# A fused decoder layer on one Trainium2 core: a prologue in halves, 26 weight pieces on GpSimd, and two steps of the end moved

## What is computed

```
x = layernorm(x + attn(x))        # causal, 32 heads of 16, with biases
x = layernorm(x + xattn(x, ctx))  # 32 query heads, 8 key/value heads of 128, rope, mask
x = layernorm(x + ffn(x))         # 4-bit weights, out = (silu(x Wg) * (x Wu)) Wd
```

## Time and profile before

| what | us |
|---|---|
| median of 3 runs | 992.58 (988.86 to 994.84) |
| the profiled execution: time / span | 994.55 / 992.7 |
| first matmul / first scores | 14.96 / 32.66 |
| self-attention, scores of step 0 to scores of step 56 | 154.0 |
| steps 56 to 71 | 73.0 |
| cross-attention and feed-forward, from 259.64 to the end | 733.1 |
| TensorE / VectorE / ScalarE / GpSimd busy in the span | 912.0 / 729.7 / 463.7 / 365.3 |

### The profile page before, as it was taken

One profiled execution on the slowest core, in us unless ns is written; L12 is line 12 of the kernel. 1 busy time (PEld: TensorE's weight loads), 2 busy tenths in 40 slices (PEclk: granted clock), 3 DMA queues, 4 the chain that ended last, 5 costly groups with the idle time before them and its releaser, 6 DMA issues.

```text
span 992.7 us, 17835 instructions
## 1 busy us (share of the span) xinstructions
PE 912.0 (92%) x6552; PEld 520.5 (52%) x6552; DVE 729.7 (74%) x1190; ACT 463.7 (47%) x1335; POOL 365.3 (37%) x330
## 2 busy tenths in 40 slices
PE   3876899888789999999999999999998989999997
PEld 2555677544345555545555555555554544444443
DVE  5685989877577877859787687787788655898343
ACT  3665788641145545535554454554545533333100
POOL 2152122103345444534554455446556230231011
PEclk9997999889999999999999999999999999999999
DMA  6634442210001101012002003004111010220001
GB/s 198 222 133 145 154 119 65 84 67 1 1 1 44 41 25 42 24 43 85 23 2 85 22 2 106 2 32 154 49 48 47 4 48 1 95 96 1 11 33 43
DMA packets 50535, 59.48 MB, mean 60 GB/s; under 512 B 5037, under 2 KB 35728, under 8 KB 50448
## 3 DMA queue, kind: packets, MB, share of 16 engines
q1 hardware_dynamic: 50448, 58.33, 18.2%
HBM read 51.96 MB, written 6.36 MB: 59 GB/s over the span
## 4 chain that ended last, share of the span: by engine, by line
PE 66%; DVE 13%; issue 9%; POOL 4%; ACT 4%; DMA 2%; SPq 1%; POOLq 0%; DVEq 0%; ACTq 0%
PE bank L292 19%; PE bank L293 19%; PE bank L294 19%; DVE rsin L873 3%; PE bank L1271 2%; ACT prob L691 1%; PE bank L1162 1%; POOL res L463 1%; DVE nmax L791 1%; PE bank L1261 1%; PE bank L1260 1%; PE bank L1259 1%; PE bank L1255 1%; DVE pTl L765 1%; ACT prob L575 1%
## 5 line engine op out<-in xcount | busy, mean ns | idle before, releaser
L470 POOL TENSOR_TENSOR rot<-rcos,rsin 128x512 f32<-128x512 f32 x80 | 101.3, 1266 | 123.2 <-DVE rsin L873 123.1
L482 POOL TENSOR_TENSOR pnrm<-prob,rden 128x512 f32<-128x512 f32 x64 | 66.5, 1040 | 125.0 <-DVE rden L933 124.9
L292 PE MATMUL bank<-aTh,xqh 128*128 128x512 f16 x256 | 98.2, 384 | 6.4 <-DVE aTl L765 3.7
L293 PE MATMUL bank<-aTl,xqh 128*128 128x512 f16 x256 | 98.1, 383 | 0.0
L530 ACT ACTIVATE pTh<-bank 128x512 f16<-128x512 f32 x128 | 78.5, 613 | 41.8 <-PE bank L1271 28.1
L294 PE MATMUL bank<-aTh,xql 128*128 128x512 f16 x256 | 97.9, 383 | 0.0
L294 PE MATMUL bank<-xoh,o2l 128*128 128x512 f16 x256 | 97.8, 382 | 0.0
L293 PE MATMUL bank<-xol,o2h 128*128 128x512 f16 x256 | 97.7, 382 | 0.0
L292 PE MATMUL bank<-xoh,o2h 128*128 128x512 f16 x256 | 97.6, 381 | 0.0
L610 ACT CAST q2h<-rot 128x512 f16<-128x512 f32 x64 | 39.5, 617 | 116.4 <-POOL rot L470 116.3
L575 ACT ACTIVATE prob<-bank,ebias 128x128 f32<-128x128 f32 x256 | 73.6, 382 | 42.3 <-DVE ebias L794 41.9
(11 more groups left out here) (159 smaller groups left out, 2454.0 us busy)
## 6 DMA issues: line engine op xcount, KB each, us to landing
tst<-tables SPq DMA_DIRECT2D x11, 768.0 KB, 5.5
xqs<-in_xwq SPq DMA_DIRECT2D x8, 1024.0 KB, 6.7
xos<-in_xwo SPq DMA_DIRECT2D x8, 1024.0 KB, 5.5
qst<-in_fq SPq DMA_DIRECT2D x11, 384.0 KB, 3.4
kstk<-stack SPq DMA_DIRECT2D x48, 64.0 KB, 2.3
qstk<-stack SPq DMA_DIRECT2D x24, 128.0 KB, 2.6
stT<-in_xT SPq DMA_DIRECT2D x4, 512.0 KB, 7.2
stT<-in_ctxT SPq DMA_DIRECT2D x1, 2048.0 KB, 8.1
```

What stands on the lines that cost most here:

```text
L292: pe.matmul(out_ap, ah, bh, start=first, stop=False)
L293: pe.matmul(out_ap, ah, bl, start=False, stop=False)
L470: nc.gpsimd.tensor_tensor(rot[:, r % 2, :], rcos[:, r % 2, :], rsin[:, r % 2, :], ALU.add).then_inc(rope_rot, 1)
L482: nc.gpsimd.tensor_tensor(pnrm[:, v % 2, :].rearrange("p (h k) -> p h k", h=QH), prob[:, v % 2, :].rearrange("p (h k) -> p h k", h=QH), rd ...
```

## The change

The prologue loads the key weights first, then the columns of x of the first four sequences in four parts of 128x512, then the query and value weights, then the other half of x. TensorE waits for one weight and for each part of x apart. ScalarE issues the DMAs of the biases, and those of the first queries' way through HBM. The high parts of the first keys and queries come straight from PSUM on ScalarE, the low parts from VectorE. `tables()` and the mask go to step 1, behind the row maximum of step 0 and ahead of that of step 1, and their loads stand on SP behind the first keys' reads.

GpSimd takes all three operations (scale, high, low) of 26 pieces: 6 of self-attention (c = 2 and 3), the 4 of the output projection, 12 of groups 0 and 1, 4 of group 0's output. Its bias additions are spread over steps 24 to 31. `ebias` of self-attention goes from VectorE to ScalarE. `v1l` is made in step n = 4 of a block, not n = 5. At the end the turning of four sequences starts one step later, and the first gate/up tile stands in step 135, not 136.

The diff, cut to what moves work:

```diff
-    plan += [(END - 6 + b, "t", (1, b)) for b in range(4)]
+    plan += [(END - 5 + b, "t", (1, b)) for b in range(4)]
-    qkv = {0: [24, 26, 28, 30, 32, 34], 1: [38, 40, 42, 44, 46, 48]}
-    out = {0: [50, 52, 54, 55], 1: [T0 + 2, T0 + 3, T0 + 4, T0 + 5]}
+    qkv = {0: [26, 28, 29, 30, 34, 36], 1: [38, 42, 44, 45, 46, 50]}
+    out = {0: [52, 53, 54, 58], 1: [T0 + 2, T0 + 3, T0 + 4, T0 + 5]}
...
+W1_SLOT = {(2, 0): 4, (2, 1): 5, (2, 2): 6, (3, 0): 20, (3, 1): 21, (3, 2): 22}
+WO1_SLOT = {0: 10, 1: 12, 2: 13, 3: 14}
+POOL_QKV, POOL_OUT = (0, 1), (0,)
...
-EARLY_GU = {END: [0], END + 1: [1], END + 3: [2], END + 5: [3]}
+EARLY_GU = {END - 1: [0], END + 1: [1], END + 3: [2], END + 5: [3]}
-GU_USE = {0: END + 1, 1: END + 2, 2: END + 4, 3: END + 6}
+GU_USE = {0: END, 1: END + 2, 2: END + 4, 3: END + 6}
...
-            load_w1(0)
-            for k in range(NK):
-                sp.dma_start(stT[:, k, :], xT[k * P:(k + 1) * P, :]).then_inc(x_in[k], 16)
-            with nc.allow_non_contiguous_dma("bias columns"):
-                for dst, src in ((ident, ident_d), (tri_f, tri_d)):
-                    sp.dma_start(dst[:, :], src).then_inc(early_in, 16)
-                for i, src in enumerate((bq, bk, bv)):
...
+            load_first_w1(0, wkT)
+            load_x(0)
+            load_first_w1(1, wqT)
+            load_first_w1(2, wvT)
+            load_x(1)
+            for dst, src in ((ident, ident_d), (tri_f, tri_d)):
+                sp.dma_start(dst[:, :], src).then_inc(early_in, 16)
             load_w1(1)
+            keep_first_keys()
+            bring_keys(0)
             for dst, src in ((cosq, cosq_d), (sinq, sinq_d), (cosk, cosk_d), (sink, sink_d), (shq, shq_d)):
...
-            stack_rows(0)
+            sp.wait_ge(xT_lo, NHALF * NK)
             sp.dma_start(stT[:, :, :], ctxT.rearrange("(k p) t -> p k t", p=P)).then_inc(ctx_in, 16)
             stack_rows(1)
...
-            for j in range(BLOCKS):
-                split_keys(j)
-                split_queries(j)
-                if j == 1:
+            def add_bias(b):
+                if b == 0:
                     pool.wait_ge(res_in, 32)
-                    for b in range(NB):
-                        nc.gpsimd.tensor_tensor(res[:, b, :], res[:, b, :], bo_bc[:, :], ALU.add).then_inc(res_ready, 1)
+                nc.gpsimd.tensor_tensor(res[:, b, :], res[:, b, :], bo_bc[:, :], ALU.add).then_inc(res_ready, 1)
+
+            pieces_done = 0
+
+            def split_piece(hi, lo, src, lo_done):
+                nonlocal pieces_done
+                pieces_done += 1
+                nc.gpsimd.tensor_scalar(src, src, 2.0 ** E_W, None, ALU.mult).then_inc(piece_scaled, 1)
+                pool.wait_ge(piece_scaled, pieces_done)
+                nc.gpsimd.tensor_copy(hi, src).then_inc(piece_hi, 1)
+                pool.wait_ge(piece_hi, pieces_done)
+                nc.gpsimd.tensor_tensor(lo, src, hi, ALU.subtract).then_inc(lo_done, 1)
...
+            for t in range(FIRST, END + 7):
+                j, n, v = t // TILES1, t % TILES1, t - T0
+                if 0 < j + 2 < BLOCKS and n == 6:
+                    split_keys(j + 2)
+                if 0 < j + 1 < BLOCKS and n == 0:
+                    split_queries(j + 1)
+                pieces(t)
+                if 24 <= t < 24 + NB:
+                    add_bias(t - 24)
                 inverse_sds(1, t)
                 for f in fills_at(t - 1):
                     if f in ROPES:
...
+                column = dict(scale=2.0 ** (E_QK - E_X - E_W), bias=bcols[:, 1, j // NHALF:j // NHALF + 1])
+                if j == 0:
+                    nc.scalar.activation(k1h[:, :], proj_bank(j, "k")[:, :], ACT.Identity, **column).then_inc(first_hi, 1)
+                nc.scalar.activation(qkf[:, 0, :], proj_bank(j, "k")[:, :], ACT.Identity, **column).then_inc(k1_f32, 1)
 
...
                 if u >= 2:
                     act.wait_ge(t_psum, u - 1)
@@ -627,11 +712,11 @@
                 split_hi(aTh[:, :, b * S:(b + 1) * S], by_k(bank[4 + b % 2][:, :]), E_X).then_inc(late_hi, 1)
 
...
+            def keep_first_queries():
+                act.wait_ge(first_lo, 2)
+                for i, src in enumerate((q1h, q1l)):
+                    act.dma_start(stack_d[0, 2 + i], src[:, :]).then_inc(q1_out, 16)
+
+            def bring_first_queries():
+                act.wait_ge(q1_out, 32)
+                for slot, part in enumerate((2, 2, 3)):
+                    act.dma_start(qstk[slot * ROWS:(slot + 1) * ROWS, 0, :, :],
+                                  stack_d[0, part].rearrange("(p r) t -> r p t", r=ROWS)).then_inc(stack_in[0], 16)
+
+            with nc.allow_non_contiguous_dma("bias columns"):
+                for i, src in enumerate((bq, bk, bv)):
+                    act.dma_start(bcol[:, i, :], src.rearrange("(c p) -> p c", p=P)).then_inc(bias_in, 16)
+            w1_split_hi(0, 0)
             for k in range(NK):
-                act.wait_ge(x_in[k], 16)
-                split_hi(aTh[:, k, :], stT[:, k, :], E_X).then_inc(xT_hi, 1)
-            act.wait_ge(early_in, 80)
+                x_split_hi(0, k)
+            w1_split_hi(0, 1)
+            act.wait_ge(bias_in, 48)
             for i, e in enumerate((E_QK, E_QK, E_V1)):
                 split_hi(bcols[:, i, :], bcol[:, i, :], e).then_inc(scaled_bias, 1)
+            w1_split_hi(0, 2)
...
+                if t == FIRST + 3:
+                    for k in range(NK):
+                        x_split_hi(1, k)
...
+                if t == FIRST + 5:
+                    keep_first_queries()
                 if j + 1 < BLOCKS and n == 4 and t > -TILES1:
                     v1_out(j + 1)
+                if t == FIRST + TILES1:
+                    bring_first_queries()
...
-                dve.wait_ge(nmax_done, u + 1)
-                nc.vector.tensor_scalar(ebias[:, u % 2, :], nmax[:, u % 2, :], 2.0 ** (-2 * E_QK) / 4, None,
-                                        ALU.mult).then_inc(ebias_done, 1)
...
+            def first_split_lo(i):
+                dst, hi, done = ((k1l, k1h, k1_f32), (q1l, q1h, q1_f32))[i]
+                dve.wait_ge(done, 1)
+                dve.wait_ge(first_hi, i + 1)
+                nc.vector.tensor_tensor(dst[:, :], qkf[:, i, :], hi[:, :], ALU.subtract).then_inc(first_lo, 1)
...
-                if t == -TILES1:
+                if t == FIRST + 2:
+                    first_split_lo(0)
+                if t == FIRST + 3:
+                    for k in range(NK):
+                        x_split_lo(1, k)
+                if t == FIRST + 4:
+                    first_split_lo(1)
+                if t == 1:
                     tables()
...
-                if before + 1 < BLOCKS and m == 4 and t - 1 > -TILES1:
-                    v1_split_lo(before + 1)
+                if j + 1 < BLOCKS and n == 4 and t > -TILES1:
+                    v1_split_lo(j + 1)
...
-                    pe.wait_ge(w1_lo, 3 * (c + 1))
+                    pe.wait_ge(w1_lo, 3 * c + 1)
+                    if j == 1:
+                        pe.wait_ge(xT_lo, NHALF * NK)
                     if j >= 1:
                         pe.wait_ge(q1_f32, j)
...
-            pe.wait_ge(xT_lo, NK)
-            pe.wait_ge(consts_ready, 4)
```

165 lines of the change are left out of this document (108 added, 57 removed).

## The result

The changed kernel takes 977.75 us (973.92 to 979.11), the kernel before, in the same comparison, 991.74 us: a ratio of 0.985 (0.981 to 0.989). The forecast was 952 us, in a range of 941 to 967. The direction was right, the size was less than half of it: 14 us instead of 40. The profiled execution has a span of 976.5 us, 16.2 us less than before.

What follows compares the result with a forecast made beforehand. TensorE works almost without a break from 259.64 us, so gains lay before that and in cross-attention's last steps. Terms summed to -41.1 us on 994.55, giving 953.4; with the runs' median 2 us lower, 952 us, range 941 to 967.

Steps and rivals of the forecast that it cites:

- first scores: Prologue: first scores at 23 us instead of 32.66, 9.7 us earlier, between 21.5 and 26.
- block 0: Between steps 1 and 2: TensorE held up 5 us by the tables, plus 1.5 us of low clock.
- block 1: Self-attention: the additions leave GpSimd, six pieces take their room; 19.5 us instead of 33.86, 14.4 us won.
- blocks 2 to 5: Self-attention: v1l waits, low clock and VectorE work fall away; 18.6, 18.6, 18.5 and 19.5 us, 9.3 us won.
- block 6: Self-attention: VectorE without three low parts and ebias; 16 us instead of 18.19, 2.2 us won.
- step 56 to 63: Behind block 6: clock of 0.78 behind waits for VectorE recovers; 4.5 us won, three quarters of what full speed would bring.
- steps 63 to 128: Stretch where TensorE already works almost without a break: forecast to stay as it is, no gain.
- the end: From step 130: later turning and earlier gate/up tile remove waits and low clock; 7.5 us won, between 5 and 8.
- the forecast's stall: Block 0: tables() ahead of step 1's row maximum holds up the exponent and TensorE for 5 us.
- rival (b): Blocks 3 to 5: GpSimd becomes the late one, some 13 us of stalls with longer pieces, 965 us; chance 0.20.
- The rule on GpSimd: VectorE instructions with two SBUF inputs and GpSimd's exclude each other; only four cTl and prologue low parts lose, 1 us each.
- Rival (d): Slower than before: each piece holds VectorE for its length whatever its inputs; +21 us, 1013 us; chance 0.02.

Runs made afterwards that it cites:

- e5_reads: e4_tables, with SP issuing the context's load (2 MB) only once the first queries' rows have landed: 979.35 us, ratio 0.988.
- e9_tables2: e5_reads, with the nine loads of the tables ahead of those of woTs and res on SP: 973.69 us, ratio 0.980.
- e14_best2: Changed kernel with the edits of e2_adds, e3_v1l, e6_w1ld, e9_tables2 and e8_guearly, but the tables in step 17: 968.40 us, ratio 0.976.
- e15_best3: e14_best2 with the six pieces of group 0 on ScalarE and VectorE: 963.73 us, ratio 0.971.
- e11_best: Changed kernel with e3_v1l, e6_w1ld, e9_tables2 and e8_guearly, additions in steps 40 to 47, xos load behind block 7's way: 972.94 us, ratio 0.979.
- e7_gu: Changed kernel with the first gate/up tile back in step 136, the turning still one step later: 979.80 us, ratio 0.988.
- e8_guearly: Changed kernel with the first gate/up tile in step 135 directly behind the scores, ahead of the turning of the weights: 977.50 us, ratio 0.986.
- e13_pieces0: Changed kernel with the six pieces of group 0 back on ScalarE and VectorE: 965.79 us, ratio 0.975.
- e16_best4: e15_best3 with the prologue, the tables in step 1 and the order of early loads as in e6_w1ld: 959.16 us, ratio 0.966.
- e1_xos: Changed kernel with SP's load of xos (1 MB) behind block 5's way through HBM instead of ahead: 972.31 us, ratio 0.980.
- e3_v1l: Changed kernel with v1l one step later again (n = 5), behind that step's row maximum and pTl: 973.31 us, ratio 0.981.
- e6_w1ld: e3_v1l, with SP issuing the weights of c = 2 ahead of the way of block 1: 968.02 us, ratio 0.976.
- e2_adds: Changed kernel with the bias additions in steps 32 to 39, behind block 5's queries, and the xos load behind block 6's way: 965.82 us, ratio 0.974.
- e12_adds_only: Kernel before, with only its eight bias additions moved on GpSimd, behind the queries of block 4 instead of block 1: 986.47 us, ratio 0.994.
- e10_ebias: Changed kernel with ebias of self-attention back on VectorE: 982.74 us, ratio 0.990.
- e4_tables: Changed kernel with tables() and the mask in step 12, their nine loads on SP behind the way of block 1: 980.24 us, ratio 0.988.

## Why the prediction was wrong, step by step

| step | forecast | profiled execution |
|---|---|---|
| first scores | -9.7 | -5.99 |
| block 0 | +6.5 | +3.20 |
| block 1 | -14.4 | -11.06 |
| blocks 2 to 5 | -9.3 | +0.16 |
| block 6 | -2.2 | -0.09 |
| step 56 to 63 | -4.5 | -1.10 |
| steps 63 to 128 | 0 | +1.62 |
| the end | -7.5 | -2.94 |
| sum | -41.1 | -16.20 |

The +1.62 of steps 63 to 128 is no effect of the change: eight other executions of the same code took 527.9 to 528.4 us there, 528.0 before. In the same eight the end would be -4.6.

**Prologue and block 0: right in sum, -3.2 forecast, -2.8 measured, and that is luck:** two misses of 3.7 and 3.3 us cancel. TensorE started at 6.86 us (forecast 7). The first scores came 3.7 us later than forecast, and the tables hid behind that. The reads of the queries ran beside the tables' loads, and in ten executions with these loads the last read landed 3.7 to 4.9 us after its issue; without them it took 2.6 to 2.8 us in e5_reads, e9_tables2, e14_best2 and e15_best3, and 4.6 us in e11_best, where the keys' reads were late as well. So the loads seem to cost 1 to 2 us. The rest of the spread of the first scores, 24.50 to 26.75 us with the same prologue, is in the issue of the reads (19.59 to 21.51 us), which waits for the queries' writes to land. e7_gu, e8_guearly, e13_pieces0 and e16_best4, with the same loads, took 23.4 to 24.5 us for block 0, and TensorE waited 3.9 to 4.3 us in it for the exponent: the forecast's stall, then in full. In three of them the scores were early; in e13_pieces0 (26.10) two operations of the tables took 0.69 and 1.26 us instead of 0.28 and 0.42.

**Blocks 2 to 5: the step that failed.** "There are about 4 us to spare, so the forecast has 1 us of stall." Two terms were mis-sized. The scaling was bounded by the cast (0.61) and the addition (1.26), with 0.7 taken "since it has one input"; it took 1.49, outside both bounds. With it a piece costs 3.4 us, not 2.7, as in rival (b), which had 3.6. And the place on SP, which the same paragraph names, was priced at nothing; e1_xos shows 4.6 us of wait for it. A third error is in the count: rival (b) gives block 3 three pieces, but the table of the diff puts four there (steps 26, 28, 29 and 30), so that even at 2.7 us a piece the block asks 24.4 us of GpSimd, not 21.7, and at 3.4 us some 27. The queries of block 5 left GpSimd 6.0 us after the start of block 4 before (134.90 less 128.86) and 15.9 us after it in the changed kernel, 9.8 us later instead of the forecast's 6; the five pieces since GpSimd's last pause, at 0.7 us more each, are most of the difference. Rival (b)'s 13 us of stalls are the 9.39 and 1.62 us measured, with the clock at 0.89 and 0.90 in blocks 4 and 5. It deserved more than one chance in five.

**v1l.** "v1l is made a step earlier, ahead of the two operations on oTh and oTl" counted what it gets ahead of, and not what it gets in front of: the row maximum. The waits for `v1l` did go (blocks 2 and 3 are at TensorE's own pace), and e3_v1l shows its price: 1.3 us in block 0, 1.4 in block 6, which is most of the 2.1 us that this block lacks, and in block 1 a wait that another one hid.

**Block 1.** The mechanism was right; the third piece did come between keys and queries. But the first piece began at 47.17 us behind the weights' load, which the forecast did not look up on SP, and the queries left GpSimd at 61.96 us where the forecast had 52. e3_v1l and e6_w1ld together bring the 19.5 us that were forecast (18.69).

**Steps 56 to 63.** The low clock stayed (0.80 where it was 0.78). I had put it down to VectorE's load; VectorE is busy 3 us less there, and the waits for `pTl` and `prob` are much the same. Ahead of the wait at 188.75 us it is `v2l` that stands before a row maximum, just as `v1l` does. That this is the cause was not tried. And the clock differs between executions of the same code here too: e2_adds, e3_v1l and e13_pieces0 took 24.3 to 24.6 us at 0.87 to 0.89, and e12_adds_only, with the steps of before, 24.64 at 0.90 instead of 27.19. So the 4.5 us forecast and the 1.1 measured both hang on it.

**The end.** "One step later the rotation is done, for 0.5 us" was true for the turning itself (0.59 us at step 131). What came late next was not asked: in step 135 the low part of the fourth turned sequence (`aTl`) now lies in front of the last output parts (`o2l`) on VectorE, and TensorE waits there. e7_gu parts the two edits: -2.6 us for the tile where 1.8 were forecast, and for the turning -0.4 us, or -2.1 without the low clock of its one execution, where 5.7 were forecast.

**ebias: right, and worth more than was said.** The forecast counted 64 times 0.17 us. With the pieces on GpSimd it would have been 0.386 at the median, and step 63 6.7 us later.

**The rule on GpSimd.** The two tiles in the changed kernel, by tile as in the earlier trace rows:

```profile
L872 DVE SCALAR_TENSOR_TENSOR cTl<-stT,cTh x4: 1216/1458/1748, 41.1 to 72.6; 128x1024 f16<-128x1024 f32 x4
```

```profile
L872 DVE SCALAR_TENSOR_TENSOR pTl<-bank,pTh x128: 672/692/693, 33.8 to 791.7; 128x512 f16<-128x512 f32 x128
```

`pTl` never took more than 0.693 us in the changed kernel and `cTl` up to 1.748 (that one began while GpSimd was in a subtraction), and a scaling that began 0.6 us behind a `cTl` took 2.47 us instead of 1.49. The Trainium skill (SBUF — State Buffer, Who interferes with whom) says that whoever issues first gets the shared ports for its whole instruction; the trace agrees, from both sides. The same section says that `tensor_scalar` can enter a two-port mode and then contends as well. I had left that out, though the earlier trace rows showed it: `ebias` has one input and took up to 0.655 us there, so the rows agreed with my shorter rule for `cTl` and `pTl` only. `ebias` is such an operation: e10_ebias agrees with the page, with 1.11 us at most, though no run shows the mode itself. Rival (d) is out: VectorE's busy time fell from 729.7 to 699.9 us.

## What to carry to other kernels

When work moves to an engine that others wait for, draw up its queue in time, with every item and its input's arrival, up to the item that the critical path needs; a sum by block hides that all the lateness may fall on one hand-over (9.39 us here), and that taking one part out of the queue may cure it. Count the items from the table itself. For an operation moved earlier, ask what now stands behind its wait, on its engine and on its DMA queue: that was the cost of `v1l`, of `xos`, of the context's load and of three of my own experiments. An unknown operation is not bounded by two others that differ from it in type or in inputs; leave its upper end open, by a factor of two. And before a span's difference is put down to an edit, look at stretches that the edit does not touch: here they differed by up to 3.4 us.

## What the runs showed of the hardware

A GpSimd scaling of 128x512 from float32 to float32 in place took 1.49 us, more than an addition of two float32 operands (1.27) or a subtraction into float16 (1.16), and 2.4 times a cast to float16 (0.61). A small VectorE operation (128x4) that takes 0.17 us alone took up to 1.11 us beside GpSimd's pieces. The reads of the first queries, three of 128 KB, landed 3.0 to 4.4 us after their issue beside small loads (the changed kernel); with 2 MB issued 0.8 us ahead of them they took 7.2 to 8.3 us, and the scores began 9.2 us after the first issue (21.90 to 31.07, e4_tables). The same prologue brought the first scores at 24.50 to 26.75 us in different executions. Behind the same wait of TensorE (1.66 or 1.67 us in step 135) the granted clock fell in two of ten executions of the same code and stayed at 1.00 in eight; where it fell, the end took 1.7 us longer.
